# Own keys' turn at the end of the third step, and another order of ScalarE's copies, in a four-layer attention kernel

## What is computed

```python
x = x + einsum('bct,bcd->bdt', x, L0_weights[cond])          # mixes 32 tokens
x = x + (x @ base.T + bias + lora(x, adapter_ids))           # linear with adapters
# attention: 4 batches x 128 rows share 32 query heads, 8 key heads, D = 128
q = rope(rmsnorm(x @ Wq)); k = rope(rmsnorm(x @ Wk)); v = x @ Wv
kc, vc = k_cache[block_table], v_cache[block_table]          # 512 cached keys
k_all, v_all = concat(kc, k), concat(vc, v)                  # plus 32 own keys
scores = where(valid, q @ k_all.T * SCALE, -1e30)
o = softmax(scores) @ v_all
x = x + o @ Wo.T
x = x + einsum('bct,bcd->bdt', x, L3_weights[cond])
```

## Time and profile before

| | |
|---|---|
| time, median of 3 runs | 2390.04 us (2388.29 to 2393.2) |
| the profiled execution | 2394.14 us, span 2392.4 us |
| busy PE / DVE / ACT / POOL | 2312.0 / 1760.8 / 1535.2 / 1395.5 us |
| granted PE clock | 0.994 of full speed |
| attention stage | about 740 to 2190 us of the span |

### The profile page before, as it was taken

How to read it: one execution, slowest core, us unless ns; L and a number is a source line. 1 busy time by engine, 2 the same in 40 slices (tenths; PEclk the granted TensorE clock), 3 DMA queues, 4 the chain that set the end, 5 groups by cost and what they waited for, 6 DMA issues and landing times.

```text
span 2392.4 us, 58277 instructions
## 1 busy us (share of the span) xinstructions
PE 2312.0 (97%) x15392; PEld 2010.2 (84%) x15392; DVE 1760.8 (74%) x5422; ACT 1535.2 (64%) x4221; POOL 1395.5 (58%) x2249
## 2 busy tenths in 40 slices
PE   8999999999998899999999999999999999998999
PEld 5778888888887788888888888888888888887777
DVE  4434777777778887887887887887887887886232
ACT  4324666666667777777777777777777777775221
POOL 1003454444447777877877877877877877872000
PEclk9999999999998999999999999999999999999999
DMA  4335333333337777777767777777767777775332
GB/s 164 95 110 163 102 98 102 111 106 102 97 115 257 221 224 239 253 228 237 255 223 241 253 228 237 255 223 242 252 220 245 253 223 241 253 221 194 110 132 101
DMA packets 347959, 455.96 MB, mean 191 GB/s; under 512 B 34506, under 2 KB 280842, under 8 KB 343695
## 3 DMA queue, kind: packets, MB, share of 16 engines
q1 hardware_dynamic: 308398, 315.83, 41.9%
q0 software_dynamic: 36864, 134.23, 16.9%
q10 hardware_dynamic: 2528, 4.29, 0.5%
HBM read 374.53 MB, written 79.69 MB: 190 GB/s over the span
## 4 chain that ended last, share of the span: by engine, by line
PE 48%; DVE 23%; issue 19%; ACT 5%; POOL 3%; DMA 1%; DVEq 0%; ACTq 0%; POOLq 0%; SPq 0%
PE S L1168 11%; PE oP L1168 11%; DVE regC L987 8%; PE S L1260 7%; DVE k_lo L284 7%; PE oP L1241 3%; PE oP L1092 3%; DVE regC L986 3%; PE S L1209 3%; PE bank L1092 2%; PE oP L1122 2%; ACT regC L721 2%; PE bank L1260 2%; DVE nmx L975 1%; DVE rinv L981 1%
## 5 line engine op out<-in xcount | busy, mean ns | idle before, releaser
L1241 PE MATMUL oP<-regC,regK 128*128 128x128 f32 x4096 | 541.2, 275 | 0.1
L1241 PEld LDWEIGHTS oP<-regC,regK 128*128 128x128 f32 x4096 | 507.2, 192 | 9.6 <-issue 0.3
L975 DVE CUSTOM_DVE_ANT_0 regC<-S,mask 128x544 f32<-128x544 f32 x512 | 368.1, 719 | 187.9 <-issue 185.7
L715 ACT CAST k_hi<-regK 128x544 fp32r<-128x544 f32 x512 | 331.3, 647 | 210.5 <-PE S L1209 184.1
L721 ACT ACTIVATE regC<-regC,nmx 128x544 f32<-128x544 f32 x512 | 384.9, 752 | 58.8 <-DVE nmx L975 49.8
L534 POOL TENSOR_TENSOR regC<-regC 128x256 f32<-128x256 f32 x320 | 244.3, 784 | 278.3 <-DVE regC L944 278.3
L549 POOL TENSOR_TENSOR q_hi<-regC,ones 128x128 fp32r<-128x128 f32 x512 | 262.3, 512 | 233.8 <-PE S L1209 229.1
L1092 PE MATMUL bank<-ident,regC 128*128 128x128 f32 x2048 | 321.1, 279 | 26.9 <-ACT regC L765 21.0
L284 POOL TENSOR_TENSOR k_lo<-regK,k_hi 128x192 fp32r<-128x192 f32 x512 | 341.4, 667 | 3.3 <-ACT k_hi L715 3.3
L987 DVE TENSOR_SCALAR regC<-regC,rinv 128x512 f32<-128x512 f32 x512 | 337.8, 660 | 0.0
L284 DVE TENSOR_TENSOR k_lo<-regK,k_hi 128x352 fp32r<-128x352 f32 x512 | 328.2, 641 | 2.9 <-ACT k_hi L715 2.9
(11 more groups left out here) (137 smaller groups left out, 4468.9 us busy)
## 6 DMA issues: line engine op xcount, KB each, us to landing
regK<-kT_cache SPq DMA_DIRECT2D x1024, 128.0 KB
qkT_d<-regC SPq DMA_DIRECT2D x160, 256.0 KB, 2.3
regC<-qkT_d SPq DMA_DIRECT2D x64, 512.0 KB
oT_d<-regC SPq DMA_DIRECT2D x64, 256.0 KB
regK<-oT_d SPq DMA_DIRECT2D x16, 1024.0 KB, 5.0
regC<-wqk SPq DMA_DIRECT2D x10, 1024.0 KB, 5.2
v_d<-regC SPq DMA_DIRECT2D x32, 256.0 KB, 2.3
regK<-qkT_d SPq DMA_DIRECT2D x64, 128.0 KB
```

What stands on the lines that cost most here:

```text
L715: nc.scalar.copy(k_hi[u % 2].rearrange("p (s t) -> p s t", t=PSIZE), k_sb[b][:, :, h, :]).then_inc(s_khi, 1)
L975: nc.vector.tensor_tensor_reduce(out=p_sb[u % 4], in0=scores, in1=mask[u // HK % 2][:], scale=-SCALE, scalar=3e38, op0=ALU.add, op1=ALU.mi ...
L1241: last = nc.tensor.matmul(oP[:, j * 512:j * 512 + P], v_sb[b][:, m, u % HK * D:(u % HK + 1) * D], pT_sb[u % 2][:, m * P:(m + 1) * P], star ...
```

## The change

The own keys' turn moves from the head of a fourth step to the tail of the step before it, `turn_p` of a fourth step from behind the value products to ahead of them, and in ACT's fourth step the order becomes copy of the turned block, `out_heads`, `exps`, where it was `exps`, `out_heads`, copy. No instruction is added or removed.

```diff
 # ScalarE, step(g, u)
-                if u % 4 == 0:
-                    if not (fixed and n + 2 >= NU):
-                        exps(n + 2, u + 2)
-                    if not (fixed and n == 0):
-                        out_heads(g, u)
                 act.wait_ge(s_ta, n + 1)
                 ge(act, s_pv, n - 1)
                 nc.scalar.copy(pT_sb[u % 2], pT).then_inc(s_evA, 1)
-                if u % 4 and not (fixed and n + 2 >= NU):
+                if u % 4 == 0 and not (fixed and n == 0):
+                    out_heads(g, u)
+                if not (fixed and n + 2 >= NU):
                     exps(n + 2, u + 2)
 # TensorE
             def turn_own(g, u):
-                pe.wait_ge(s_evA, g * UG + u)
-                nc.tensor.transpose(pT[:, 0:P], po_sb[(u - 4) // 4 % 2], ident[:]).then_inc(s_tb, 1)
+                pe.wait_ge(s_evA, g * UG + u + 1)
+                nc.tensor.transpose(pT[:, 0:P], po_sb[u // 4 % 2], ident[:]).then_inc(s_tb, 1)
 # TensorE, step(g, u)
-                if u % 4 == 0 and not (fixed and n == 0):
-                    turn_own(g, u)
                 if not (fixed and n + 2 >= NU):
                     score(n + 2, u + 2)
-                if u % 4:
-                    turn_p(g, u)
+                turn_p(g, u)
                 of = g if u >= UG - 2 else before
                 if u in WO_AT and WO_AT[u] < H2 and of is not None:
                     out_proj(of, WO_AT[u], WO_AT[(u + 1) % UG])
                 if u > 0:
                     values(g, u - 1)
                 elif not (fixed and n == 0):
                     values(g - 1, UG - 1)
-                if u % 4 == 0:
-                    turn_p(g, u)
+                if u % 4 == 3:
+                    turn_own(g, u)
```

More of the change, by code:

```diff
@@ L1312, in _ @@
                 step(NT - 1, u, None)
-            turn_own(NT - 1, UG)
             values(NT - 1, UG - 1)
```

## The result

The changed kernel takes 2409.30 us (median of 4 runs, 2406.61 to 2409.78), the kernel before 2389.59 us (median of 4). The ratio is 1.0078 (95% interval 1.006 to 1.0095): 0.8% slower. The profiled execution took 2409.78 us with a span of 2408.0 us, 15.6 us longer than the one of before.

The account below looks back on a forecast made before the run. It took PE, busy 97% of the span, as the bound. Pairs' +0.72 us and knock-on's +0.4 made 1.12 us for each of 16 turns, +18 us on 2390.04: 2408 us; forecast case 2400 to 2422, stated range 2390 to 2428.

Parts of the forecast that it names:

- The chain: Fourth step and the next: late exponentials delay DVE's maximum by 0.83 us; the pair takes 5.33 us instead of 5.19.
- One sign: Expected in the profile: exponentials start some 0.8 us later in fourth steps, directly behind the heads' copy.
- The seven pairs: Fourth steps other than u = 0, each with the step behind it: 0.14 us slower each, +0.98 us a turn.
- u = 0: First pair of a turn, with output projection between: late maximum hidden, faster turn gains 0.26 us.
- The knock-on: Four pairs with POOL gathers: DVE's late normalising is caught by them, 0.1 us each, +0.4 us a turn.
- The own keys' turn: Its move from the fourth step's head to the third's tail: same order on PE, cost 0, gain 0.
- The gathers' rival: Late normalising waits for the gather's end at four pairs: 2.9 us a turn, +47 us, 2437; chance 0.15.
- Absorbed: Lateness of pairs ahead of a wait for POOL disappears in it: 0.3 us a turn, +5 us, 2395; chance 0.14.
- Faster: Scores do not wait for DVE's late maximum: 1.9 us a turn gained, -30 us, 2360; chance 0.08.

Follow-up runs that it names:

- e9: The changed kernel itself, unaltered, run on the second chip: 2404.32 us, ratio 1.0057 to the kernel before.
- e12: The kernel of e1 with the own keys' turn back at the head of the fourth step, on the second chip: 2384.02 us, ratio 0.9972.
- e10: The changed kernel with the own keys' turn back at the head of the fourth step, on the second chip: 2405.56 us, ratio 1.0064.
- e1: The changed kernel with ACT's order copy of the turned block, exponentials, heads in all fourth steps: 2387.83 us, ratio 0.9991.
- e4: The order of e1 and the early turn only in fourth steps with u % 8 == 0; those with u % 8 == 4 as in the kernel before: 2379.83 us.
- e11: The kernel of e4 with the own keys' turn at the head of the fourth step, on the second chip: 2378.29 us, ratio 0.9948.
- e2: The changed kernel with ACT's old order (exponentials, heads, copy), so PE's part of the change alone: 2427.89 us, ratio 1.0159.
- e3: The changed kernel with PE's old order (turn behind the products), so ACT's part of the change alone: 2454.91 us, ratio 1.027.
- e6: The kernel of e4 with two of the four gathers issued one step earlier, on the second chip: 2403.93 us, ratio 1.0058.
- e8: The kernel of e1 with two of the four gathers issued one step earlier, on the second chip: 2409.09 us, ratio 1.0078.

## Why the prediction was right

The time (2408 against 2409.3) and the direction came out, and in the steps u = 8, 16 and 24 the mechanism did. In the steps with u % 8 == 4 the prediction left out a link of the chain, and that the sum came so near is partly luck. By its steps:

*The chain.* Offsets from the scores at 1497.28, the predicted ones in brackets: turn 0.94 (1.03), products 1.43 (1.46), own products 2.42 (2.44), next scores 2.85 (2.87), heads 2.99 (3.09), exponentials 3.47 (3.56), reciprocal 4.34 (4.45), maximum 4.43 (4.53), scores 5.31 (5.33). Two terms were off and cancelled: the heads' wait was 0.57 instead of the 0.65 read from u = 0 (both values occur, by the step), and the scores start 0.88 behind the maximum, where I had estimated 0.80. PE goes on 0.06 us behind ACT's small copy (1498.16 to 1498.22), not 0.14, but most of that is gone by the products, which start 0.49 behind the turn and not 0.43. One sign was wrong in size: the exponentials start 1.50 us later than before (3.47 against 1.97), not "some 0.8"; the chain itself said 1.59.

*The seven pairs.* On the second chip, e9 against the kernel before: u = 4, 8, 12, 16, 20, 24, 28 cost 0.20, 0.11, 0.09, 0.19, 0.09, 0.30, 0.08, together 1.06 us (predicted 0.98, each 0.14). I had read one pair and multiplied. Pairs 16 and 24 were shorter before (5.02 and 5.04) and so had more to lose. u = 0 gained 0.23 (0.26).

What I left out is DVE's low part of the heads, which stands ahead of the reciprocal at u = 4, 12, 20 and 28. At u = 12 it had put the maximum at 4.03 already in the kernel before, so the maximum is 0.40 us late in e9 (4.43) and not 0.83. The scores still follow it by 0.88, but a second limit lies just below: in e12, with the exponentials early, these pairs are 5.26 us and not 5.22, because the value products wait for the low part. So of the 0.09 us at u = 12 the late exponentials account for 0.05.

*The knock-on.* The 0.4 us for gathers that catch DVE's late scaling is the term that failed: the steps behind the pairs changed by 0.02 us at most in e9. The catching itself happened, but PE did not see it. At u = 12 of e9 the scaling of the own keys' columns (L983) lasts 0.64 us and ends at 1510.55, as the gather does (1510.57); the rest of the scaling ends at 1510.83, and PE's turn starts at 1510.98, 0.84 behind its scores, which is its own pace. Before, the turn had come 0.69 us behind the end of the scaling (1505.03, from the earlier trace rows):

```profile
1504.35 0.29 DVE L986 TENSOR_SCALAR regC<-regC,rinv 128x32 f32<-128x32 f32 x1
...
1505.72 0.60 PE L1092 MATMUL bank<-ident,regC 128*128 128x128 f32 x4
```

The delay used up that room and no more. What the chip of the first profile added in its place, 0.25 us a tile at u = 28, has another cause, and that the period grew by 1.03 us there, near the 1.12 predicted, is the luck. On the second chip the same kernel costs 0.79 us a tile, 13.7 us in all. That lies in the forecast's own range, at its lower part.

*The own keys' turn.* Priced at nothing, and it costs nothing (e9, e10).

*The rivals.* The gathers' rival (2437) did not happen. The Trainium skill says in "SBUF — State Buffer", "Who interferes with whom", that of VectorE in a two-port mode and GpSimd the one that issues first holds the shared ports for its whole instruction and blocks the other. The 0.64 us of L983, which ends with the gather, agree with that; the scaling at 1504.56 in the earlier trace rows does not, for the gather was first there (1504.42) and the scaling still took its usual 0.47 us. So that row does not show, as I had written, that the order of the two decides. The low keys are no evidence either way: they took 0.78 us also at 1505.30 in e9, where no gather ran. Absorbed (2395): the waits for POOL at u = 15 and 23 swallowed only what the late cast added, not the 0.1 us of pairs 12 and 20. Faster: it needed a maximum 0.39 us earlier. e1 and e4 show that at u = 8, 16 and 24 this rival was one swap of two calls away: with the exponentials ahead of the heads the maximum of u = 8 starts 1.07 us behind its scores and the pair is 4.96 us, near the 4.94 that the prediction named as PE's own pace.

## What to carry to other kernels

When an engine's queue is reordered, look for the one instruction with the long wait and ask what now stands behind it. The stall that the profile named (53 waits, 15.3 us) was really removed, and the time went up, because the exponentials were moved behind the heads' copy; put into that wait instead, they hold up nothing at u = 8, 16 and 24. Two places of a pattern that look alike can have different limits (here DVE's low part of the heads in every second one), so a new order is worth trying for each kind of place by itself: e4 and e11 are 0.5% faster than before, e1 and e12, with the same order everywhere, 0.1 and 0.3%.

## What I had not expected

The same kernel had ACT's cast start 0.74 to 0.84 us behind the own products in most tiles at u = 12, 20 and 28 on the chips of its first profile and of e1 and e2, and 0.57 us everywhere on the chip of e9, with instruction streams and neighbours alike to 0.02 us. e3 has it too, in another instruction: at u = 12, 20 and 28 ACT's copy starts 0.90 to 0.98 us behind the turn in most tiles, and 0.69 at u = 8 and 16. It moved the median by 5 us (2409.3 and 2404.3) and e1's by 3.8 (2387.8, and 2384.0 for e12, whose own keys' turn is at the head), while the kernel before read the same on both (2391.0, 2390.6): there the cast waits for the exponentials and hides it. What differs between the chips is open. And a gather issued one step earlier was dear for a reason far from where it was moved: up to 3.6 us of waiting for a sequence's key pages, and in e6 and e8 a lower clock behind half of these waits.
